# A Mamba stage on one core: mixing ahead of the convolution on VectorE, time steps later, and one ScalarE copy moved up

## The reference

```
proj = layernorm(x) @ in_proj_w.T                   # z (1024), xBC (1280), dt_raw (16)
xBC  = silu(causal_conv_4_taps(xBC) + conv_b)
x_ssm, B, C = split(xBC)                            # 1024, 128, 128
dt   = softplus(dt_raw + dt_bias);  A = -exp(A_log)
Y    = ssd_scan(x_ssm * dt, dt * A, B, C, block 64) + x_ssm * D
y    = Y * silu(z);  y = y / rms(y) * norm_w
x    = x + y @ out_proj_w.T
```

## Time and profile before

| | us |
|---|---|
| median of three runs (lowest, highest) | 1653.71 (1653.46, 1655.51) |
| the profiled execution's own time | 1658.66 |
| its span in the trace | 1657.0 |
| Mamba turns, 7 with inputs to prepare | from 785 to 1273.6 |

### The profile page before, as it was taken

How to read it: one execution, slowest core, us unless ns; L and a number is a source line. 1 busy time by engine, 2 the same in 40 slices (tenths; PEclk the granted TensorE clock), 3 DMA queues, 4 the chain that set the end, 5 groups by cost and what they waited for, 6 DMA issues and landing times. The chain is left out here.

```text
span 1657.0 us, 34129 instructions
## 1 busy us (share of the span) xinstructions
PE 1515.7 (91%) x11983; PEld 1267.6 (76%) x12004; DVE 927.4 (56%) x2133; ACT 720.9 (44%) x1784; POOL 597.7 (36%) x473
## 2 busy tenths in 40 slices
PE   6999999998799999978799999999999879999997
PEld 5788788787498879966667678776777558888896
DVE  4677777776622234215787786877868662222222
ACT  3666666666032234325454455554455302222222
POOL 5556556555223334430232222333223302333342
PEclk9999999999799999989899999999999869999999
DMA  5356455444589777532001101011000037787753
GB/s 211 118 183 207 145 181 204 157 166 160 200 274 315 220 223 189 86 63 73 14 20 34 46 26 33 21 33 44 24 25 21 32 128 268 195 264 195 185 91 56
DMA packets 95918, 212.36 MB, mean 128 GB/s; under 512 B 7217, under 2 KB 7217, under 8 KB 94513
## 3 DMA queue, kind: packets, MB, share of 16 engines
q1 hardware_dynamic: 76736, 166.58, 28.8%
q0 software_dynamic: 17472, 40.90, 12.5%
q10 hardware_dynamic: 1584, 3.15, 0.5%
HBM read 136.94 MB, written 73.66 MB: 127 GB/s over the span
## 5 line engine op out<-in xcount | busy, mean ns | idle before, releaser
L1298 PE MATMUL bank<-ring,halves 128*128 x1872 | 331.9, 326 | 3.5 <-ACT halves L1137 3.5
L1298 PEld LDWEIGHTS bank<-ring,halves 128*128 128x128 f32 x1872 | 302.6, 188 | 10.7 <-issue 4.5
L498 POOL TENSOR_TENSOR arena<-arena 128x1024 f32<-128x1024 f32 x64 | 123.8, 1935 | 142.1 <-DVE arena L578 140.5
L1696 DVE SCALAR_TENSOR_TENSOR arena<-arena 128x256 f32<-128x256 f32 x240 | 136.9, 612 | 17.8 <-ACT arena L1916 14.9
L1147 ACT ACTIVATE arena<-bank 128x512 f32<-128x512 f32 x78 | 46.7, 598 | 210.0 <-DMA mid_rows<-arena 74.1
L1592 POOL TENSOR_TENSOR arena<-arena 128x1024 f32<-128x1024 f32 x16 | 31.4, 1960 | 274.7 <-ACT arena L1970 236.3
L791 PE MATMUL bank<-arena 128*128 128x128 f32 x1024 | 124.7, 281 | 1.8 <-ACT arena L691 0.8
L710 ACT ACTIVATE arena<-arena 128x256 f32<-128x256 f32 x256 | 126.4, 500 | 0.0
L791 PEld LDWEIGHTS bank<-arena 128*128 128x128 f32 x1024 | 118.8, 194 | 7.7 <-issue 3.6
L1109 POOL DMA_INDIRECT arena<-normalised_rows,arena x78 | 80.5, 1032 | 101.2 <-PE bank L1281 49.1
L1117 POOL DMA_INDIRECT out_dram<-arena x39 | 61.8, 1585 | 152.8 <-issue 104.5
(11 more groups left out here) (285 smaller groups left out, 3301.7 us busy)
## 6 DMA issues: line engine op xcount, KB each, us to landing
ring<-expert_halves SPq DMA_DIRECT2D x16, 4352.0 KB
expert_halves<-expert_high SPq DMA_DIRECT2D x16, 1088.0 KB, 8.7
expert_halves<-expert_rest SPq DMA_DIRECT2D x16, 1088.0 KB, 11.0
arena<-in_w_dram SPq DMA_DIRECT2D x8, 1088.0 KB, 7.0
normalised_rows<-arena SPq DMA_DIRECT2D x33, 256.0 KB, 2.0
arena<-in_x_dram SPq DMA_DIRECT2D x32, 256.0 KB, 2.8
arena<-mid_rows SPq DMA_DIRECT2D x32, 256.0 KB, 2.8
w_in_raw<-in_in_w_dram SPq DMA_DIRECT2D x16, 290.0 KB
```

What stands on the lines that cost most here:

```text
L498: nc.gpsimd.tensor_tensor(held, held, spread(rinv[:, HG * g:HG * g + HG], 2, 2 * P), ALU.mult)\
L1298: last = nc.tensor.matmul(bank[1 + 2 * par + part][:, 0:INTER], rows_parts[a][:, par, k * P:k * P + P], weights(at, b, (2 * k + part) * IN ...
L1696: last = nc.vector.scalar_tensor_tensor(out=slot[:, j], in0=cin[:, c, k:k + PAIR], scalar=taps[:, c, k:k + 1], in1=slot[:, j], op0=ALU.mul ...
```

## The change

In the odd tile, on VectorE, `mix` and `first_block` come ahead of the convolution of unit 2 instead of behind it; `time_steps`, which stood between `first_block` and `second_block`, comes behind `scored.normalise`, ahead of the convolution of unit 4. On ScalarE the copy `scored.turned_out` comes ahead of the SiLU of the last unit ("the fourth", counted from 0), not behind it.

```
@@ VectorE, odd tile
                 mean_of(t - 1)
                 rest_of_y(t - 1)
-                if front:
-                    convolve(link, n, 2)
                 mix(t)
                 first_block(t)
                 if front:
-                    time_steps(link, n, 1 - pp)
+                    convolve(link, n, 2)
                 second_block(t)
                 if front:
                     convolve(link, n, 3)
...
                 scored.normalise(dve, t - 1, xres)
                 if front:
+                    time_steps(link, n, 1 - pp)
                     convolve(link, n, 4)
                 rows_done(link, t, 1)
@@ ScalarE, odd tile
                     conv_in(n, 4)
+                scored.turned_out(act, t - 1, bank[7])
+                if front:
                     conv_out(n, 4, 1 - pp)
-                scored.turned_out(act, t - 1, bank[7])
                 if front:
                     gate(t + 1, 0)
```

## The result

The changed kernel takes 1649.47 us (median of 20 runs, 1644.38 to 1655.55), the kernel before 1656.06 in its 20. The ratio of their undisturbed runs is 0.9964, 95% interval 0.9949 to 0.9978: about 6 us less, 0.36%. One of the 20 runs of before took 3359.17 us and doesn't enter the ratio. The forecast was 11.6 us less. A second set of runs, with the first experiment, gave 0.9947 (0.9928 to 0.9965).

The account below looks back on a forecast made before the run. TensorE bounds the kernel, VectorE the odd tile after the change. 12.0 us of slack plus 7 x 0.3 make 14.1, less 2.5 for the clock 11.6: from 1653.71 to 1642.1 us, range 1632 to 1650.

Parts of the forecast that it names:

- The waits: TensorE's four odd-tile waits at L2213, L2190, L226 and L238, 3.67 us in sum, all go.
- the two new ones: TensorE at the next turn's start waits 0.7 us at L2142 and another 1.6 at L2149.
- the walk: Step-by-step timing of the reordered odd tile of turn 5, giving a gain of 1.3 us in such a turn.
- VectorE's gain on y: VectorE's rows y in the odd tile are ready at 1205.2 instead of 1205.49, 0.3 us earlier a turn.
- add 7 x 0.3: VectorE's 0.3 us in each of seven turns, added to 12.0 us of slack at the gate product.
- the sum without a fall: Gain over seven turns before any cost of clock falls: 14.1 us.
- The clock: At the turns' starts, falls that count in half of seven turns at 0.68 us each, about 2.5 us.
- the bound I had named: Upper bound on the cost of clock falls at turn starts: seven at 1.56 us, 10.9 us.
- The third rival: Clock falls behind L2149 every turn and again in the even tile, 21.8 us against 14.1: 1661; chance 0.05.
- The first rival: TensorE stays the bound, L2149 doesn't wait: up to 30.9 us gained, 1622.8; chance 0.10.
- The second: Odd tile's mixing held through both GpSimd operations, L1602 and L1606; y 1.6 us later, no change, 1653; chance 0.07.
- The rule on the clock: TensorE's activity is judged in free-running windows, so instruction order can't give the number of falls; gain 14.1 to 3.2 us.

Follow-up runs that it names:

- the first experiment: The changed kernel run once more, unaltered, against the kernel before: ratio 0.9947 (0.9928 to 0.9965).
- The fills: Changed kernel with unused TensorE products in its waits at L2142, at L2149 or at both; ratios to the kernel before 0.9877, 0.9944 and 0.9908.
- both filled: Changed kernel with 4 unused TensorE products ahead of L2142 and 6 ahead of L2149; ratio to the kernel before 0.9908.

## Why the prediction was half right

**The waits, right.** Each of the four went whole, and the two new ones are where and as long as the walk had them, for the reason given: L2142 waits for L1779, L2149 for L1784.

**VectorE's gain on y, too small.** The walk gave 0.3 us a turn. In the changed kernel L2200 starts at 967.48 and y ends at 991.94, 24.46 behind it; before it was 1205.49 - 1180.18 = 25.31. That is 0.85 us. Of the 0.55 us between the two 0.44 is convolution 2, which was held for L1610 alone (4.36 us and not 4.8); the rest of L1606 did not hold it. With this the step "add 7 x 0.3" becomes 7 x 0.85, and the sum without a fall 18.0 us instead of 14.1. The fills measured just that: 508.0 - 490.0 = 18.0, and 17.4 with both filled.

**The clock, the step that failed.** "I take a fall that counts in half of the seven turns at the cheaper price of 0.68, about 2.5 us": it fell in all seven, in three for twice as long, and cost 501.3 - 490.6 = 10.7 us, 1.5 a turn. That is about the bound I had named, 10.9, and I had gone by the number of microseconds waited, 3.67 before and 2.3 after. The fills show the size of the waits to be the wrong measure: with 0.84 us open beside the small products there were six falls, with 1.36 us open behind them none. The two errors, +3.9 and -8.2 us, turn 11.6 into 7.3; S says 6.8 and the timed runs 6.

**The number.** The forecast of 1642.1 us started from 1653.71, the median of three runs; the 20 runs gave 1656.06, 2.35 us more. So 1649.47 is 7.4 us over the forecast, 5 of them by the smaller gain. It lies inside the stated range only because its upper end had the bound of the clock's cost in it.

The third rival had the mechanism, a fall at the start of every turn, and its sign came: seven falls against five, and a granted clock of 0.959 against 0.963 in the profiled executions. It had the wrong price: one fall a turn and not two. The first rival's condition, no wait at L2149, did not come. The second, the mixing held twice, did not happen in the odd tiles.

**The rule on the clock.** From the windows that run freely in the Trainium skill ("TensorE: Matmul & The Clock Gate", Part 1, "What's actually happening") the prediction drew that the number of falls can't be had from the order of instructions. Two traces of the changed kernel don't bear this out: they have the same seven falls, the same three of them long, and S within 0.3 us. But the two also agree in the fall at the start of turn 0, and across all traces that one moved against the stage by up to 2.6 us, with the same instructions ahead of it. That shift fits the rule. What it does to the falls behind the change is not shown here, neither way.

## What to carry to other kernels

When TensorE is nearly always busy, price a wait by what the granted clock does behind it, in the trace, and not by its length: some 8 us, by the timed runs, came from moving one 0.6 us copy ahead in ScalarE's queue. Read the falls of more than one trace before you trust their number. Where a wait can't be removed, a few unused products in it can cost nothing and hold the clock (10.7 us here). Before moving work within a queue, ask which engine sets the end of the turn after the move, and put the moved work where that engine stands idle: the same time steps gave S 501.3 behind the normalised row and 483.0 at the start of the tile (with ScalarE's exponential moved as well).

## What the runs showed of the hardware

- At the starts of turns a fall of the clock lasted 3.4 or 6.8 us, once 10.2 (VectorE's part only), and 13.7 in the last turn; once at half, the clock stayed there over 4 us and more in which TensorE had no pause (1061 to 1065 in the stretches above).
- The place and the length of a fall go into its price: six falls of 3.4 us that begin at L2142 or in the wait ahead of it cost 7.1 us (497.7 against 490.6), the seven of the changed kernel, three of them twice as long, 10.7.
- VectorE and GpSimd pass each other between operations: the mixing, issued during L1602, ran ahead of L1606, which then took 2.89 us; the convolution issued with L1610 took 4.36 us against 2.71 alone, 1.65 for GpSimd's 2.08.
